# Sampling loop: TensorE's sum of three taps copied by ScalarE, six taps added by GpSimd

## The reference

```
xin = einsum('bchw,oc->bohw', x, in_proj_w)
xc  = silu(dwconv3x3(xin))
x1  = gelu(layer_norm(dwconv3x3(xc)))
offset = x1 @ off_w.T + off_b              # 2 numbers per pixel and channel group
xs  = bilinear sample of xc at (pixel + offset), 4 taps by weight
Bs, Cs, dts = x_proj(xs)
delta = softplus(dt_w @ dts + dt_bias);  dA = exp(delta * A);  dBx = delta * Bs * xs
h_t = dA_t * h_(t-1) + dBx_t;   y = h * Cs + Ds * xs
x   = x + out_proj(layer_norm(y))
```

## Time and profile before

| | |
|---|---|
| median of 3 runs | 2626.13 us (2622.99 to 2626.7) |
| the profiled execution | 2632.59 us, its span 2630.7 us |
| busy over the span | TensorE 2209.4 us, VectorE 1954.1, ScalarE 1457.5, GpSimd 1419.7 |
| additions of GpSimd, line 900 | 320, 407.3 us, mean 1273 ns |
| products of VectorE, line 816 | 576, 379.1 us, mean 687 ns |
| first and last addition of VectorE, line 861 | 799.2 us and 2468.2 us, 64 of them, 677 to 690 ns |

### The profile page before, as it was taken

The page is one execution under the profiler, slowest core; times in us unless marked ns, Lnnn a source line. Parts: engine busy times, 40 slices in busy tenths (PEclk is TensorE's granted clock), DMA queues, the critical chain, the costliest instruction groups (busy, mean ns, idle before and its releaser), DMA issues.

```text
span 2630.7 us, 29183 instructions
## 1 busy us (share of the span) xinstructions
PE 2209.4 (84%) x7671; PEld 1139.9 (43%) x7671; DVE 1954.1 (74%) x3324; ACT 1457.5 (55%) x2268; POOL 1419.7 (54%) x1223
## 2 busy tenths in 40 slices
PE   3898769897978989986988977889899689899788
PEld 2397525343433333332335964454344233333233
DVE  6556746598967999994765667566889499999754
ACT  1743533485765676663346436237677466766532
POOL 2231019387857888872322400475778388888532
PEclk9988879899989999998997988899999799999989
DMA  4000463400000010014720008333000001001145
GB/s 175 1 1 0 150 215 105 167 1 0 0 1 1 17 33 17 16 33 122 236 46 1 0 1 288 117 104 128 0 0 1 2 1 32 17 21 29 51 119 120
DMA packets 131749, 155.96 MB, mean 59 GB/s; under 512 B 4951, under 2 KB 107743, under 8 KB 128247
## 3 DMA queue, kind: packets, MB, share of 16 engines
q1 hardware_dynamic: 131575, 154.00, 19.1%
HBM read 81.69 MB, written 72.29 MB: 59 GB/s over the span
## 4 chain that ended last, share of the span: by engine, by line
PE 42%; DVE 25%; issue 12%; POOL 8%; ACT 7%; DMA 3%; SPq 1%; DVEq 1%; ACTq 0%; POOLq 0%
PE PSUM L2190 7%; POOL BIG L900 6%; PE PSUM L701 6%; PE PSUM L2011 4%; DVE BIG L816 3%; DVE BIG L840 3%; PE PSUM L2246 3%; PE PSUM L2054 3%; PE PSUM L2252 2%; PE PSUM L2068 2%; PE PSUM L2210 2%; DVE BIG L847 2%; DVE PSUM L823 2%; DVE BIG L1082 2%; DVE BIG L861 2%
## 5 line engine op out<-in xcount | busy, mean ns | idle before, releaser
L900 POOL TENSOR_TENSOR BIG<-BIG 128x512 f32<-128x512 f32 x320 | 407.3, 1273 | 108.3 <-DVE BIG L861 86.1
L816 DVE TENSOR_TENSOR BIG<-PSUM,BIG 128x512 f32<-128x512 f32 x576 | 379.1, 687 | 74.1 <-PE PSUM L1010 31.1
L1082 DVE SCALAR_TENSOR_TENSOR PSUM<-BIG,VECS,PSUM 128x1024 f32<-128x1024 f32 x240 | 309.2, 1288 | 43.8 <-PE PSUM L2011 37.4
L742 POOL TENSOR_TENSOR BIG<-TOEP,BIG 128x384 f32<-128x384 f32 x84 | 97.2, 1183 | 342.7 <-DVE BIG L1484 342.7
L1010 PE MATMUL PSUM<-BIG,SELB 120*128 120x512 bf16 x576 | 211.6, 387 | 82.6 <-DVE BIG L816 74.7
L2011 PE MATMUL PSUM<-BIG,WDW 128*128 128x512 f32 x576 | 263.5, 604 | 11.3 <-ACT BIG L1920 11.3
L1718 POOL TENSOR_SCALAR BIG<-BIG,VECS 128x1024 f32<-128x1024 f32 x64 | 181.3, 2845 | 50.6 <-DVE PSUM L1542 50.6
L2190 PE MATMUL PSUM<-BIG 128*128 128x381 f32 (+1 forms) x576 | 190.1, 494 | 15.2 <-DVE BIG L749 15.2
L1016 PE MATMUL PSUM<-BIG,CSTS 128*128 128x512 f32 x384 | 202.4, 609 | 0.0
L1010 PEld LDWEIGHTS PSUM<-BIG,SELB 120*128 120x128 bf16 x576 | 56.0, 98 | 277.4 <-DVE BIG L816 185.1
L2011 PEld LDWEIGHTS PSUM<-BIG,WDW 128*128 128x128 f32 x576 | 108.2, 192 | 141.5 <-issue 126.9
(11 more groups left out here) (362 smaller groups left out, 5366.5 us busy)
## 6 DMA issues: line engine op xcount, KB each, us to landing
spill<-X SPq DMA_DIRECT2D x18, 1024.0 KB, 6.3
back_spill<-BIG SPq DMA_DIRECT2D x32, 576.0 KB, 3.4
X<-x SPq DMA_DIRECT2D x32, 512.0 KB, 7.6
rows_spill<-X SPq DMA_DIRECT2D x64, 256.0 KB, 4.2
out<-BIG SPq DMA_DIRECT2D x64, 256.0 KB, 3.6
BIG<-rows_spill SPq DMA_DIRECT2D x28, 512.0 KB, 5.1
X<-back_spill SPq DMA_DIRECT2D x14, 896.0 KB, 11.7
BIG<-fc SPq DMA_DIRECT2D x8, 1024.0 KB, 9.7
```

The source lines that it names most:

```text
L742: eng.tensor_tensor(to.rearrange("p (x c r) -> p x c r", x=3, r=WROW), TOEP[:, y].unsqueeze(1).unsqueeze(1).broadcast_to([P, 3, WCH, WROW] ...
L816: dve.tensor_tensor(img(o), img(PSUM[:, (k + q) % 2, :]), pch(c, XBASE, dy, dx), ALU.mult).then_inc(df_p, 1)
L900: pool.tensor_tensor(XS[:, k, :], XS[:, k, :], product_buffer(q), ALU.add).then_inc(df_add, 1)
L1082: return dve.scalar_tensor_tensor(out=rows8(to), in0=strip(c, base, dy, dx), scalar=vc(weights, j), in1=rows8(acc), op0=ALU.mult, op1=ALU.add)
```

## The change

XS gets its first value from ScalarE: once TensorE's sum of taps 0 to 2 is there (df_acc), and the old tile's reader is done (sc_y), ScalarE copies bank ACC to XS and signals df_xs. This copy stands in ScalarE's queue behind line 952 and ahead of line 957. VectorE's addition (line 861) goes. The product of tap 3 goes to a buffer like those of taps 4 to 8, and GpSimd adds six products in place of five; the product of tap 5 and with it the third addition move ahead of line 909, and the sixth stands last, ahead of line 925. VectorE's waits for free buffers are renumbered: products 3 to 5 wait for additions 3 to 5 of the tile before, products 6 to 8 for additions 0 to 2 of their own tile.

```diff
--- before.py
+++ after.py
@@ -776,14 +776,14 @@
 
             return T * n + (m + 1 + CREDIT)
 
-        PE_SUMS, POOL_SUMS = PE_TAPS, NTAP - 1 - PE_TAPS
+        PE_SUMS, POOL_SUMS = PE_TAPS, NTAP - PE_TAPS
 
         def product_buffer(q):
 
-            n = q % 2 if q < PE_TAPS else 2 + (q - PE_TAPS - 1) % 3
+            n = q % 2 if q < PE_TAPS else 2 + (q - PE_TAPS) % 3
             return SPARE if n == 4 else PRD[:, n, :]
 
-        assert POOL_SUMS == 5
+        assert PE_SUMS == 3 and POOL_SUMS == 6
 
         def sample_and_scan_dve(dve, pair, stats):
             dve.memset(W9, 0.0).then_inc(df_zero, 1)
@@ -798,21 +798,15 @@
                         return
                     dy, dx = TAPS[q]
                     dve.wait_ge(df_w, turn(T, q))
-                    if q == PE_TAPS:
-
-                        dve.wait_ge(sc_y, reuse(T))
-                        o = XS[:, k, :]
+                    if q < 2:
+                        dve.wait_ge(df_acc, summed(T - 1, PE_SUMS - 1 - (PE_SUMS - 1 - q) % 2, PE_SUMS))
+                    elif q < PE_TAPS:
+                        dve.wait_ge(df_acc, summed(T, q - 2, PE_SUMS))
+                    elif q < PE_TAPS + 3:
+                        dve.wait_ge(df_add, summed(T - 1, q - PE_TAPS + 3, POOL_SUMS))
                     else:
-
-                        if q < 2:
-                            dve.wait_ge(df_acc, summed(T - 1, PE_SUMS - 1 - (PE_SUMS - 1 - q) % 2, PE_SUMS))
-                        elif q < PE_TAPS:
-                            dve.wait_ge(df_acc, summed(T, q - 2, PE_SUMS))
-                        elif q < PE_TAPS + 4:
-                            dve.wait_ge(df_add, summed(T - 1, 3 if q == PE_TAPS + 1 else 4 if q == PE_TAPS + 2 else 2, POOL_SUMS))
-                        else:
-                            dve.wait_ge(df_add, summed(T, q - PE_TAPS - 4, POOL_SUMS))
-                        o = product_buffer(q)
+                        dve.wait_ge(df_add, summed(T, q - PE_TAPS - 3, POOL_SUMS))
+                    o = product_buffer(q)
                     dve.tensor_tensor(img(o), img(PSUM[:, (k + q) % 2, :]), pch(c, XBASE, dy, dx),
                                       ALU.mult).then_inc(df_p, 1)
 
@@ -854,11 +848,6 @@
                     far_dve(dve, c - 1, (k + 1) % 2, reach)
                 product(3)
                 product(4)
-                if on(0):
-
-                    dve.wait_ge(df_acc, summed(T, PE_SUMS - 1, PE_SUMS))
-                    dve.wait_ge(df_p, turn(T, PE_TAPS))
-                    dve.tensor_tensor(XS[:, k, :], XS[:, k, :], PSUM[:, ACC, :], ALU.add).then_inc(df_xs, 1)
                 product(5)
                 product(6)
                 product(7)
@@ -891,7 +880,7 @@
                 T = pair * NT + c
                 def add(m):
                     if on(0):
-                        q = PE_TAPS + 1 + m
+                        q = PE_TAPS + m
                         pool.wait_ge(df_p, turn(T, q))
                         if m == 0:
                             pool.wait_ge(df_xs, after(T))
@@ -901,13 +890,13 @@
 
                 add(0)
                 add(1)
+                add(2)
                 if on(-1):
 
                     pool.wait_ge(sc_delta, after(T - 1))
                     pool.wait_ge(sc_bx, after(T - 2))
                     pool.wait_ge(df_add, summed(T - 1, POOL_SUMS - 1, POOL_SUMS))
                     pool.tensor_tensor(UU, RL, XS[:, (k + 1) % 2, :], ALU.mult).then_inc(sc_u, 1)
-                add(2)
                 if on(2):
 
                     pool.wait_ge(df_hat, after(T + 2))
@@ -919,6 +908,7 @@
                     ins.then_inc(df_w9, 1)
                 add(3)
                 add(4)
+                add(5)
                 if on(2):
 
                     pool.wait_ge(df_hi, after(T + 2))
@@ -950,6 +940,11 @@
                     act.activation(part(0), w9h, ACT.Copy).then_inc(df_hi, 1)
                     act.wait_ge(df_r1, after(T + 1))
                     act.activation(part(1), w9h, ACT.Copy).then_inc(df_mid, 1)
+                if on(0):
+
+                    act.wait_ge(df_acc, summed(T, PE_SUMS - 1, PE_SUMS))
+                    act.wait_ge(sc_y, reuse(T))
+                    act.activation(XS[:, k, :], PSUM[:, ACC, :], ACT.Copy).then_inc(df_xs, 1)
                 if on(2):
 
                     act.wait_ge(df_w9, after(T + 1))
@@ -1099,7 +1094,7 @@
         def _(dve):
             credit(dve, sp_log, sp_mx, sp_sub, sp_sum, sp_rec, sp_aff, sp_e, sp_acc, mh_qm, mh_mx, mh_nmx,
                    mh_rec, mh_pn, mh_vm, o_e, o_x, cv_vector, cv_part, cv_done)
-            credit(dve, sc_delta, df_p, df_xs, sc_bx, sc_h, sc_hc, sc_y, sc_t, sc_x)
+            credit(dve, sc_delta, df_p, sc_bx, sc_h, sc_hc, sc_y, sc_t, sc_x)
             dve.reg_mov(far_dve_step, 0)
             dve.reg_mov(far_dve_turn, 0)
             dve.wait_ge(load, 16 * 9)
@@ -1733,7 +1728,7 @@
         @block.scalar
         def _(act):
             credit(act, l1_sq, sp_stage, sp_pixt, sp_exp, mh_exp, mh_ptc, o_at)
-            credit(act, df_abs, df_hat, df_hi, df_mid, df_wt, sc_abs, sc_exp, sc_ln, sc_da, sc_sq, sc_lv, sc_rs)
+            credit(act, df_xs, df_abs, df_hat, df_hi, df_mid, df_wt, sc_abs, sc_exp, sc_ln, sc_da, sc_sq, sc_lv, sc_rs)
             act.wait_ge(load, 16 * 9)
             act.wait_ge(const_dve, 9)
             act.activation(SM[:, 10:11], vc("A_logs"), ACT.Exp).then_inc(const_act, 1)
```

## The result

The changed kernel takes 2656.56 us (median of 4 runs, 2653.55 to 2660.49), the kernel before 2626.2 us. The ratio is 1.0123 with an interval of 1.0106 to 1.0140, 28 to 37 us slower. Forecast were 2651 us and a range of 2638 to 2668. Its profiled execution took 2657.5 us with a span of 2655.5. The 2657.5 us are 24.9 us over the profiled execution before; the sum in the prediction was 24.5. The medians differ by more, 30.4 us.

What follows compares the result with a forecast made beforehand. The prediction took VectorE as the bound before and a 12.61 us ScalarE ring after: 62 x 0.37 = 22.9 us plus 1.6 at pair ends, 24.5 on 2626.13, gives 2651 us, range 2638 to 2668.

Steps and rivals of the forecast that it cites:

- two busy shares: In the sampling loop, VectorE's busy share falls from 95% to 87% and GpSimd's rises from 83% to 90%.
- the queue's bare length: GpSimd's new queue per step, with no wait other than 0.58 us for ScalarE: 12.51 us.
- the cover: GpSimd's idle time per step before its first addition, 1.18 us, set against 1.59 us of added work.
- That closes a ring that did not exist before: Line 847 to the next step's 847 through ScalarE's copy, lines 957 to 979 and VectorE's 823: 12.61 us, the longest.
- a sign to look for: In the changed loop, VectorE gains waits in front of products 6 to 8 for additions; no size given.
- So VectorE bounds the loop: Before the change, VectorE at 95% busy sets the 12.24 us step, with GpSimd close behind.
- 11.64 us for VectorE without 861: VectorE's step once line 861 goes, taken at 0.60 us less than 12.24.
- rival 3: VectorE stays the bound at 11.64 us a step and the kernel is faster, 2589 us; chance 0.04.
- TensorE gets no instruction more: On TensorE, projections shift with the last addition, idle share grows a little, transposes wait for the copy; no added time.
- Rival 1: Only GpSimd's queue binds, step 12.51 us, 2641 us; chance 0.15.
- Rival 2: ScalarE's ring is longer through a dearer copy, steps 12.75 to 13.13 us, 2658 to 2681 us; chance 0.21.
- Rival 4: GpSimd's cover is just enough, step stays 12.24 us, 2626 us; needs an addition of 1.18 and a free copy; chance 0.04.

Runs made afterwards that it cites:

- e5: The changed kernel run again unaltered, beside more runs of the kernel before: 2655.33 us, ratio 1.0106.
- e4: The changed kernel with product buffers dealt otherwise, products 4 and 5 using TensorE's two: 2644.17 us, ratio 1.0070.
- e2: The kernel before with an extra ScalarE copy of X onto itself at the new copy's place, waiting for line 847, unused by anyone: 2636.95 us, ratio 1.0040.
- e9: The changed kernel with the hat functions moved ahead on ScalarE, to where it waits anyway: 2652.44 us, ratio 1.0081.
- e1: The changed kernel with UU moved in front of the third addition on GpSimd: 2906.14 us, ratio to the kernel before 1.1044.
- e6: The changed kernel with e4's buffers, e9's ScalarE order, the copy ahead of line 952 and line 927 behind the next step's first addition: 2642.03 us, ratio 1.0067.
- e7: The kernel before with only its buffers dealt otherwise, so no product waits for an addition of its own tile: 2615.55 us, ratio 0.9961.
- e8: e7 with hat functions ahead of line 952 on ScalarE and tap 5's spread ahead of TensorE's third projection: 2607.27 us, ratio 0.9922.
- e3: The kernel before with a sixth GpSimd addition (ninth product added twice), no ScalarE copy, VectorE's addition kept: 2693.55 us, ratio 1.0250.
- e10: e6 with the spread of tap 5 ahead of the third projection on TensorE: 2625.7 us, ratio 0.9994.

## Why the prediction was right

**The sum.** The step was forecast at 12.61 us and is 12.61 us; the whole at 24.5 us against the profiled execution's own time and is 24.9. The direction, the range and the two busy shares held. By the medians the difference is 30.4 us; e5 shows that the loop accounts for 25 to 26 of them. That the step agrees to the hundredth is partly luck, as follows.

**GpSimd.** The term was right: the queue's bare length, 12.51 us, is 12.52 in e4. What carried the forecast was that a chained addition costs 1.41 us, that moving the third addition next to the second makes one more of them, and that the cover was 1.18 us.

**ScalarE.** The step of the prediction that did not hold is this one: "That closes a ring that did not exist before", with the sum 12.61, named as the longest. The ring exists (e2: it alone costs 0.19 us a step), but it is 12.47 us in the changed kernel and e9 shows that it does not bind. It was mis-sized by 0.14 us: hand-over to ScalarE 0.09 for 0.03, copy 0.50 for 0.48, 957 to 979 5.25 for 5.21, 823 to 847 5.36 for 5.33 (the hand-over to 823, 0.03 for 0.04, was good). The 0.09 and 0.50 are what e1 and e6 show, where ScalarE stands idle before the copy (line 839 of e6 ends at 979.63, the copy starts at 979.72, the next instruction at 980.21). With them the ring would be 12.55 us, still under 12.61. What binds instead is GpSimd's queue with 0.09 us more for product 7, whose wait for the second addition the prediction named only as a sign to look for, and gave no term. Two errors of about 0.1 us cancelled, which is luck.

**The copy's price.** 0.58 us, and 0.48 to the next start, against the 0.50 taken from line 945. The Trainium skill, "ScalarE: Activation LUTs", "Rules for kernel authors", budgets about 0.3 us plus about 0.83 ns per element for an activation whose bias is a [128,1] pointer operand, by estimate 0.72 us for 512 elements. The copy has no such operand, so that row does not price it; the activations of this size that have one and read PSUM as the copy does, 959, 961 and 972 of the changed kernel, take 0.67, 0.66 and 0.68 us.

**What bounds the kernel now.** "So VectorE bounds the loop" was wrong. At 95% busy it looked so, but e7 and e8 give VectorE the same work and the loop is faster. Before, the step of 12.24 us was a ring: first addition, second addition, product 8, 823, 847, products 3 and 4, 861, first addition, 12.22 us. The rows before show VectorE held twice in it:

```profile
972.29 0.69 DVE L816 TENSOR_TENSOR BIG<-PSUM,BIG 128x512 f32<-128x512 f32 x1 [0.24 <-POOL BIG L900]
```

This is product 7, behind the first addition. Product 8 (973.70) starts 0.10 us after the second addition's end (970.91 + 2.69) and 0.81 after the delta, where 0.60 is plain. e7 takes this ring out and the step falls. So the prediction's 11.64 us for VectorE without 861, and rival 3's 2589 us that rests on it, were too high: about 11.6 us are VectorE's work with 861 (e8). Taking 861 out of the ring would have shortened it (argued, not run alone); the added addition lengthened another.

**TensorE.** "TensorE gets no instruction more" is true and was too little. Product 5 waits 0.97 us a step for its spread in the changed kernel (all products together 0.02 before), and in e3 this wait closes the binding ring.

**Rivals.** Rival 1 (GpSimd's queue only) had the right mechanism with 2641 us, short of product 7's 0.09; e4, which takes these 0.09 away, is that rival as a kernel and took 2644.17. Rival 2 (a longer ring on ScalarE, 2658 to 2681 us) is only 1.4 us above the median measured, but its mechanism is not there: the ring is shorter than taken, and TensorE's clock stayed at 1.00. Rival 3 (VectorE stays the bound, 2589 us) would have needed the work on GpSimd to cost under 0.58 us; e6 and e10, which open the other rings that I had found, still come out at 12.52 and 12.16 us a step. Rival 4, the cover just enough, failed at 1.59 against 1.18.

## What to carry to other kernels

In a loop over several engines the step is the longest ring through their queues and waits, divided by the number of steps that it takes to come round; write down every ring through the changed instructions, those of two steps too, and look at two neighbouring steps of a trace, not one. A busy share of 95% does not prove the bound: dealing the same buffers in another order gained 10 us here, and two moves of order another 8. A chained instruction costs more than its duration (1.41 against 1.27 us on GpSimd), so where an addition stands among its neighbours counts as much as whether it is there.

## What the hardware showed that I had not expected

TensorE's clock fell in the stretch from 900 to 1160 us in e1, and in that kernel only. In most of its steps there, matmuls ran at 1.2 GHz for a part of the step, the granted clock over a step was 0.80, and the step was 17.1 us, not 15.0. The same pause of 2.79 us stood in front of steps of either kind, so what decides is not shown. In the kernels with steps up to 13.3 us it stayed at 1.00 in the same stretch.

GpSimd's additions did not suffer from the change: mean 1273 ns before, with VectorE 95% busy, and 1271 after, at 87%.

ScalarE's copy started 0.03 us after the VectorE instruction that it waits for in e2, where ScalarE was busy until then, and 0.09 us after it in e1 and e6, where ScalarE stood idle. The copy of e2 reads SBUF and the others read PSUM, so these runs don't separate the two.
